# GpSimd's low halves of layer 0's weights in pieces of 256 columns, and y's halves ahead of the output weights

## What is computed

```python
# _bi_wkv(x, f, f, w, u, cond): forward and backward scans over time
a = a * decay + ek_t * v_t ;  b = b * decay + ek_t          # for each channel
num = nf + nb - ekv + euk * vf ;  den = df + db - ek + euk
base = sigmoid(r) * (num / maximum(den, 1e-8)) ;  y = base * (0.8 + 0.2 * tf)
# _nsa_forward(y, Wq, Wk, Wv, Wg, Wo): 16 heads of 128
q, k = rope(y @ Wq), rope(y @ Wk) ;  v = y @ Wv ;  g = sigmoid(y @ Wg)
o = o_cmp * g_cmp + o_slc * g_slc + o_swa * g_swa           # three softmaxes a head
x1 = x + o @ Wo
```

## Time and profile before

| | us |
|---|---|
| median of 3 runs | 2349.98 (2349.69 to 2356.46) |
| the profiled execution, its own time | 2363.0 |
| its span, first to last instruction | 2361.3 |
| TensorE busy | 2007.7 (85%) |
| VectorE busy | 1677.1 (71%) |
| ScalarE busy | 1339.4 (57%) |
| GpSimd busy | 1099.6 (47%) |
| GpSimd, 18 low halves of head weights (L621) | 62.5, 3470 ns each |
| GpSimd, 4 low halves of output weights (L641) | 9.3 and 9.0, 4661 and 4509 ns each |

### The profile page before, as it was taken

One profiled execution on the slowest core, in us unless ns is written; L12 is line 12 of the kernel. 1 busy time (PEld: TensorE's weight loads), 2 busy tenths in 40 slices (PEclk: granted clock), 3 DMA queues, 4 the chain that ended last, 5 costly groups with the idle time before them and its releaser, 6 DMA issues. The chain is left out here.

```text
span 2361.3 us, 41986 instructions
## 1 busy us (share of the span) xinstructions
PE 2007.7 (85%) x14177; PEld 1235.3 (52%) x14177; DVE 1677.1 (71%) x3496; ACT 1339.4 (57%) x3199; POOL 1099.6 (47%) x758
## 2 busy tenths in 40 slices
PE   0579888999999999999994579966789898978999
PEld 0345555565666656666662545534566666643444
DVE  7688788888888888877763359954677778653770
ACT  4576667566566666556553324325676768646442
POOL 5576667566566656555441136644232223210440
PEclk9999999999999999999997589987889899978999
DMA  4223333221213212222123854455333334326110
GB/s 175 76 94 94 96 104 112 83 86 63 82 65 107 74 64 68 79 82 74 51 73 128 351 224 141 146 190 175 125 117 121 105 122 137 130 85 216 41 36 22
DMA packets 110015, 260.51 MB, mean 110 GB/s; under 512 B 10672, under 2 KB 39472, under 8 KB 107824
## 3 DMA queue, kind: packets, MB, share of 16 engines
q1 hardware_dynamic: 90320, 208.85, 26.1%
q10 hardware_dynamic: 16992, 41.43, 5.1%
q0 software_dynamic: 2560, 8.39, 1.0%
HBM read 179.46 MB, written 76.02 MB: 108 GB/s over the span
## 5 line engine op out<-in xcount | busy, mean ns | idle before, releaser
L830 PE MATMUL ps_q<-a_y,a_w 128*128 128x512 f16 x1536 | 344.7, 381 | 0.0
L625 POOL TENSOR_TENSOR a_rb<-a_rb,a_rot 128x512 f32<-128x512 f32 x129 | 215.8, 1673 | 270.6 <-ACT a_rb L736 270.1
L830 PEld LDWEIGHTS ps_q<-a_y,a_w 128*128 128x128 f16 x1536 | 148.9, 98 | 177.7 <-issue 4.2
L848 PE MATMUL ps_s<-a_kk,a_q 128*128 128x512 f32 (+3 forms) x512 | 194.9, 490 | 38.8 <-POOL a_kk L629 35.2
L270 DVE TENSOR_TENSOR_SCAN wkv_bwd<-wk_decay,wkv_tail,wkv_fwd 128x512 f32<-128x512 f32 x114 | 201.4, 1791 | 0.1
L883 PE MATMUL ps_g<-a_o,a_wo 128*128 (+1 forms) x768 | 179.2, 384 | 6.8 <-POOL a_o L616 4.4
L837 PEld LDWEIGHTS ps_v<-a_w,a_y 128*128 128x128 f16 x3072 | 176.9, 98 | 15.1
L837 PE MATMUL ps_v<-a_w,a_y 128*128 128x128 f16 x3072 | 182.0, 219 | 0.0
L872 PE MATMUL ps_o<-a_tt_,a_v 128*128 128x512 f32 (+3 forms) x512 | 159.6, 456 | 13.1 <-ACT a_tt_ L756 10.4
L972 DVE TENSOR_REDUCE a_nmax<-ps_s 128x1 f32<-128x512 f32 (+3 forms) x256 | 125.3, 489 | 60.1 <-PE ps_s L850 51.1
L746 ACT ACTIVATE ps_s<-ps_s,a_nmax 128x512 f32<-128x512 f32 (+3 forms) x256 | 125.2, 489 | 60.1 <-DVE a_nmax L974 53.3
(11 more groups left out here) (286 smaller groups left out, 4815.7 us busy)
## 6 DMA issues: line engine op xcount, KB each, us to landing
a_w<-wqkv_split SPq DMA_DIRECT2D x48, 768.0 KB, 4.4
scratch_numlog<-wkv_nl ACTq DMA_DIRECT2D x40, 512.0 KB, 2.7
wkv_kt<-in_fT ACTq DMA_DIRECT2D x58, 256.0 KB, 2.7
a_wraw<-in_wqkv SPq DMA_DIRECT2D x18, 768.0 KB, 5.3
wqkv_split<-a_w SPq DMA_DIRECT2D x17, 768.0 KB, 6.8
a_stacks<-qk_parts SPq DMA_DIRECT2D x96, 128.0 KB
gate_up<-in_gate_up SPq DMA_DIRECT2D x8, 1408.0 KB, 14.1
a_nlc<-scratch_numlog SPq DMA_DIRECT2D x18, 512.0 KB, 4.9
```

What stands on the lines that cost most here:

```text
L625: pool.tensor_tensor(rb[:, n, :], rb[:, n, :], rot[:, 2 * n + 1, :], ALU.mult).then_inc(s["roped"], 1)
L830: mm = pe.matmul(psq[n][:], w16[:, i % 2, wp, n, c, :], y16[b % 2][:, yp, c, :], start=c + m == 0, stop=c == CC - 1 and m == 2)
L848: pe.matmul(cols(ps, j, -lead), q[:, j * P:(j + 1) * P], kk[:, NBLK - lead:NBLK + P * (j + 1)], start=True, stop=False)
```

## The change

`split` on GpSimd makes a head's low half in six instructions of 256 columns (three matrices, two halves of each) instead of one of 1536; the semaphore is raised by the last. A new `wo_low` makes a chunk of output weights' low half in eight instructions of 256 columns instead of one of 2048. In the prologue GpSimd's `y_low` and ScalarE's `y_high` stand ahead of the output weights in every chunk, where before they did so only in the last. The split is the same function in the prologue and in the first batch, so eighteen of them are cut up. TensorE's, DVE's and SP's instructions and all arithmetic stay.

```diff
 # GpSimd
 def split(g, i):
     pool.wait_ge(s["whi"], g + 1)
-    pool.tensor_tensor(w16[:, i, 1], wraw[:], w16[:, i, 0], ALU.subtract).then_inc(s[f"w_ready{i}"], 16)
+    for n in range(3):
+        for c in (0, CC // 2):
+            piece = slice(c, c + CC // 2)
+            low = pool.tensor_tensor(w16[:, i, 1, n, piece], wraw[:, n, piece], w16[:, i, 0, n, piece],
+                                     ALU.subtract)
+    low.then_inc(s[f"w_ready{i}"], 16)
+
+def wo_low(c):
+    pool.wait_ge(s["wo_hi"], c + 1)
+    for h in range(G):
+        for n in (0, C // 2):
+            piece = slice(n, n + C // 2)
+            low = pool.tensor_tensor(wo_part(1, c)[:, h, piece], wo_raw[c % 2][:, h, piece],
+                                     wo_part(0, c)[:, h, piece], ALU.subtract)
+    low.then_inc(s["wo_lo"], 1)
...
-    if c == CC - 1:
-        y_low(0, c, c)
-    pool.wait_ge(s["wo_hi"], c + 1)
-    pool.tensor_tensor(wo_part(1, c), wo_raw[c % 2][:], wo_part(0, c),
-                       ALU.subtract).then_inc(s["wo_lo"], 1)
-    if c < CC - 1:
-        y_low(0, c, c)
+    y_low(0, c, c)
+    wo_low(c)
 # ScalarE
     y_invert(c)
-    if c == CC - 1:
-        y_high(0, c, c)
+    y_high(0, c, c)
...
-    if c < CC - 1:
-        y_high(0, c, c)
```

## The result

| | us |
|---|---|
| kernel before, median of 6 runs | 2356.82 (2349.69 to 2366.41) |
| changed kernel, median of 6 runs | 2377.42 (2373.34 to 2382.19) |
| ratio, 95% interval | 1.0094 (1.0074 to 1.0114) |
| the profiled executions, their own time | 2363.0 before, 2382.12 after |

That is +22 us by the ratio (+17 to +27) and +20.6 by the medians, where +13.8 had been forecast. The direction was right, the size was not, and 2377 lies above the range.

A forecast was written before the change was run, and what follows sets the result against it. Bound by the prologue's DVE-GpSimd exclusion and the first batch's chain through GpSimd's split to a_kk. Heads +10.4, clock +5.0, prologue -1.6 gave +13.8 us, 2363.8 us on the median; range 2350 to 2372.

The forecast's parts named there:

- Price of a piece: GpSimd subtractions: 0.63 us per 256-column piece, 0.15 us for each further instruction; bounds 0.52 and 0.67 us.
- The chain to a_kk: First batch's sixteen heads: the split delays the rotated key a_kk the scores await, 0.65 us a head, +10.4 us (8.8 to 12.0).
- TensorE's clock: First batch: longer a_kk waits put three more heads at the low clock, 1.67 us each, +5.0 us (0 to 8.4).
- The prologue: Before the first gates matmul: two weight and four output-weight subtractions in pieces, -1.6 us, middle of +1.1 and -4.3.
- The account of the held pair: Prologue: DVE and GpSimd exclude each other for whole instructions; holdings fill 48.0 of 51.4 us, despite DVE's 19.4 us of waits.
- rival C: Prologue: eight output-weight pieces with DVE in between hold up the next chunk's ekv, +5 over forecast, 2369 us; chance 0.10.
- its account of SP's queue: Prologue: later wo_lo holds back chunk 3's x and the third head's weights, each issued over 10 us early; 0.
- y's halves first: First three prologue chunks: y's halves ahead of the output weights, 0 by itself.
- The level: Whole time: +13.8 us put on the profiled 2363.0 us gives 2376.8; the same difference on the median 2349.98 gives 2363.8.
- A: Rival: pieces nearly free at 0.52 us, heads and DVE's prologue waits shrink, -8.6 us, 2341.4 us; chance 0.11.
- B: Rival: no difference, clock holds, +4.5, 2354.5 us; chance 0.22. Beside head times, B instead means scores to next projection.
- D: Rival, prologue and heads: DVE doesn't get in between pieces, which only add, +21.7 us, 2371.7 us; chance 0.07.

The follow-up runs named there:

- e1: Kernel before with the first batch's sixteen weight subtractions in six pieces of 256 columns, prologue as it was: 2382.89 us, ratio 1.0118.
- e3: As e1, but each first-batch weight subtraction in three pieces of 512 columns; against the kernel before: 2368.48 us, ratio 1.0043.
- e5: As e1, but each first-batch weight subtraction in twelve pieces of 128 columns; against the kernel before: 2399.46 us, ratio 1.0198.
- e4: Kernel before with each first-batch split, whole, moved on GpSimd behind the turning of the next head's key: 2333.33 us, ratio 0.9903.
- e6: As e4, but the moved splits in pieces of 256 columns; against the kernel before: 2337.29 us, ratio 0.9922.
- e9: Changed kernel plus eight useless TensorE matmuls before the scores in heads 1 to 15 of the first batch: 2362.66 us, ratio to before 1.0031.
- e2: Changed kernel with its prologue part kept and the first batch's sixteen subtractions whole: 2356.49 us, ratio to the kernel before 1.0000.
- e7: e2 with GpSimd's prologue output weights moved behind the next chunk's ekv, second head's split behind y's low half: 2352.97 us, ratio to before 0.9995.
- e11: Kernel before with only the changed kernel's prologue order (y's halves ahead of output weights), every subtraction whole: 2356.22 us, ratio 1.0000.

## Why the prediction was right in sign and wrong in size

- **Price of a piece**: right. 0.63 us, in the trace of after where nothing stands between; 0.14 to 0.15 us for a further instruction (e1, e3, e5), 0.15 forecast. The bounds of 0.52 and 0.67 were not needed.
- **The chain to a_kk**: the mechanism was right (e4, e6), the term a little small. +10.4, bounds 8.8 to 12.0, against 10.9 in fifteen heads and 1.6 in the sixteenth, 12.5, just outside. The a_kk waits came to 39.0 us, as forecast. The working took off 0.1 to 0.2 us a head for better handovers between GpSimd and DVE. Heads 5, 9 and 13 grew by 0.89 (16.28 for 15.39), more than five instructions cost, the others of the fifteen by 0.45 to 0.84, and the mean is 0.72: there was next to no such discount.
- **TensorE's clock**: the step that failed. +5.0 with bounds of 0 and 8.4 against +14.4 in fifteen heads. It chose the heads that would fall by the length of their wait and let three fall, those with a wait close to the 2.5 us seen before, at the 1.67 us of the earlier trace rows (B of 4.58 for 2.91). Of these three, two fell and cost 2.8 us each; the third waited 3.13 us and stayed at the full level (B of 2.91, the window shown above). Five others fell at 1.7 us each, so that the head of the earlier trace rows, expected at 18.9 to 19.1 us, took 20.88 (273.60 to 294.48). Against the same head in e9, five of the fifteen were long in before, by some 1.7 us each, and eleven are in after, seven by 1.6 to 1.7 and four by 2.8 to 2.9 us (5.69 for 2.91), among them heads with a wait of 2.12 and 2.21 us. The length of the wait alone thus doesn't say which head falls, and what else does stays open. The prediction had the warning in it: two heads low after shorter waits. Its upper bound should have been all ten heads then at the full level, 17 us at 1.67 each, not five. With head 16's 4.7 us taken off, 9.7 us net are left; but head 16's B differs among the kernels with whole splits (10.2, 6.5, 6.5 and 7.2 us in before, e2, e7 and e11), so the net figure is good to a few us.
- **The prologue**: -1.6 forecast, 0.0 at the gates, 0 in e2. The account of the held pair was right in kind: 19.4 us of visible waits were worth nothing as such. It missed that the order could have used 3.6 us (e7), and that each of DVE's short instructions now meets a piece (7.1 us for 4.3 in the last chunk). Of the two waits that came instead it named only one, ekv behind the pieces, in rival C. The other it did not see: its account of SP's queue spoke of the transfers behind wo_lo, and not of the second head's weights behind the first split (3.52 us of ScalarE).
- **y's halves first**: 0 forecast, 1.0000 in e11.
- **The level**: before's median rose from 2349.98 in the three runs shown to 2356.82 in six. Of the 13.6 us between 2363.8 and 2377.4, 6.8 are that, and 6.8 are the change's size.
- **Rivals**: A fell with the price of a piece. B was out with the clock. C named a wait that came (2.35 us for ekv), but no time was lost by it, since the waits saved covered it. D was wrong: a waiting DVE instruction gets in between two pieces (1.23 for 3.67).

## What to carry to other kernels

Cutting a GpSimd instruction up lets DVE in at each boundary, at 0.15 us a boundary for GpSimd. That can pay where DVE is what the path waits for (3.6 us at the gates in e7's trace, none shown in the whole time), and costs where GpSimd's own next result is: read who waits for whom behind the instruction, not how long the other engine is blocked. And a chain that grew by 0.72 us a head cost TensorE about twice that, since its clock fell in more of the heads: sum the work at both levels of the clock for the upper bound. The better edit was one of order, the next key's turning ahead of work that nobody waits for yet.

## What the runs showed of the hardware that I had not expected

TensorE's granted clock depends on what fills its waits, to the size of the change itself. Eight matmuls without use, 1.9 us in the head shown and put into each of fifteen, raised the clock of the stretch from 0.91 to 0.98 and made the changed kernel some 15 us faster. I had also not expected how straight the price of GpSimd's instructions is: 0.148, 0.143 and 0.139 us for each further one at 512, 256 and 128 columns, with DVE's scans going by in between in each case.
